# Graph attention in another order on VectorE and GpSimd, scores in two pairs of PSUM banks, and a mixer with ScalarE taps and full-width skip products

## The chip, the core and the metric

The kernel is one program on one core of a Trainium2 chip. TensorE (PE) does matrix products into PSUM, VectorE (DVE) and ScalarE (ACT) work elementwise, GpSimd (POOL) does elementwise work and issues indirect DMAs, and SyncE (SP) issues the other transfers. The engines run side by side and meet at semaphores. The metric is the device time of the core in microseconds (us), the median of the runs.

## What is computed

The input is `x` of 8 graphs x 1024 nodes x 128 features with an adjacency matrix of 1024x1024 each. Four blocks add to it: a graph convolution, a mixture of experts, the attention over graphs below, and a slicing block with a mixer. Two of them are touched.

```python
# attention block, per graph: 4 heads of 32, node_feats = layernorm(x)
X = heads(lrelu(node_feats @ W_lin + b_lin)); q = heads(lrelu(node_feats @ W_q)); k = heads(lrelu(node_feats @ W_k))
adj_h = adj[:, None] * sigmoid(q @ k.T * hd ** -0.5)
deg = sum(adj_h, -1); dis = where(deg > 0, deg ** -0.5, 0)
Y = (dis[..., :, None] * adj_h * dis[..., None, :]) @ X        # then layernorm(Y) * ln_g + ln_b
# mixer, inside the slicing block: 8 sequences of 64 steps, 8 heads of 64
xBC = silu(sum(xp[:, k:k + L] * conv_w[:, k] for k in range(3)) + conv_b)      # causal, 3 taps
h = h * exp(dt * A) + dt * B * x;  y = h @ C                   # scan, both directions
y = y + x_og * repeat(x_og @ fcD_w.T + Dp, 64)                 # the skip
yg = y * silu(z);  out = rms(yg) * norm_w @ out_w.T
```

## The kernel before

The stages run one after the other: convolution and experts up to about 666 us, `attention_gnn_stage` to about 1206, slicing, `hydra_stage` (the mixer) from about 1388 to 1475, and the way back to nodes.

**Attention.** A graph is 16 steps n: two halves of 512 queries by 8 tiles of 128 keys. In step g (over all graphs) TensorE does, in this order: `products` of the step 18 earlier (L1327, into YA), `scores` (L1314, four heads of 32 rows side by side in the array, into the one PSUM tile S of four banks), `degrees` of the step two earlier (L1341), and at most one side job out of the table `SIDE`: the projections k, q and x, transposes of X and Y, all through the one PSUM bank M. ScalarE makes AH (128x2048) with one sigmoid over S (L1417); the next scores wait for it (`att_ready`). VectorE multiplies AH by the adjacency tile A (L1447). AH has 18 buffers and A four. Beside the multiply VectorE has the small work of a graph in an order written out by hand, by n: the leaky functions of q, k and x (L1532, L1543), the degrees (L1490), XT = XR scaled by the degrees (L1500, `scale_X`), the statistics of the next X (`stats_x`, at step 4 for graphs 0 and 1, else at the start; for the first three graphs it adds the two gathered halves first, L1453 and L1455), and the norm of Y of the graph two earlier: `scale_Y` L1508, `stats_y`, `gain_Y`, `finish`.

GpSimd's order in a graph i: four gathers of graph i+2 (`gather`, L1242, indirect DMAs of routed expert rows), the reciprocal root of the variance of X (`norm_in.power`, L136), `root` of the degrees' second half (L1234), four gathers, R plus shift (L1287), `norm_y.power`, eight gathers, `root` of the first half, and `combine` (L1251, L1254), which adds the gathered halves and X for graph i+2 where i+2 is at least 3.

**Mixer.** TensorE projects the input, VectorE adds the three taps of the causal convolution (`convolve`, L2250 to L2254) for BC and four tiles of X, the decays go through ScalarE (L2209) and a transfer to DRAM and back into `decay`, whose ends GpSimd clears (L2090). VectorE scans twice (L2312, L2317), multiplies by G in 16 pieces (L2321), adds both directions (L2326) and applies the skip (L2332). The skip's products (L2141) take two columns of `fcD` at a time, each broadcast to 64 columns of the array, by four tiles of X.

## Time and profile before

| | us |
|---|---|
| median of 3 runs | 1538.24 (1538.18 to 1538.66) |
| the profiled execution | 1539.02 |
| its span, first to last instruction | 1537.30 |
| attention stage within it (666 to 1206) | 540 |
| mixer within it (1388 to 1475) | 87 |

The time is that of the whole launch; the profile shows one execution, 0.78 us above the median, with 1.72 us outside its span. TensorE is busy 91% of the span, VectorE 66%, ScalarE 49% and GpSimd 47%. The granted TensorE clock is 0.984 on average. Starts are in us from the span's start.

### The profile page before, as it was taken

The numbers are of one execution on the slowest core, as the hardware profiler recorded it, in microseconds if no ns is written. First come the engines' busy times: TensorE is split into PE (matmuls) and PEld (weight loads), VectorE is DVE, ScalarE is ACT, GpSimd is POOL, SyncE is SP. The second block draws the span as 40 slices with busy tenths as digits, with TensorE's granted clock in tenths as the row PEclk, the third lists the DMA queues.
The fourth block names the chain that finished last, engine by engine and source line by source line (L and its number), as shares of the span: only waits on it lengthen the run. The fifth ranks groups of instructions, "written<-read, shape, count | busy, mean of one in ns | idle before, by whom it ended". The sixth has DMA issues, their size and how long they took to land. (4 is left out here: it accounts for less than half of the span.)

```text
span 1537.3 us, 25067 instructions
## 1 busy us (share of the span) xinstructions
PE 1401.7 (91%) x9010; PEld 808.8 (53%) x9010; DVE 1021.2 (66%) x2212; ACT 748.2 (49%) x1184; POOL 720.7 (47%) x500
## 2 busy tenths in 40 slices
PE   4999999899999999977899988998999779999998
PEld 2455545669999998732222222222222357773488
DVE  2467767633333333368788999999987789967732
ACT  3365565534444444446454554655554457872110
POOL 1127776740000000749787887876233479981000
PEclk9999999999999999999999999999999999999999
DMA  9757637276788775633342424423322231004024
GB/s 300 254 188 282 235 118 228 88 205 203 229 230 231 233 228 159 171 118 125 96 129 90 124 84 122 142 84 119 91 90 69 69 95 42 15 1 90 1 85 138
DMA packets 207599, 215.26 MB, mean 140 GB/s; under 512 B 23269, under 2 KB 164709, under 8 KB 207476
## 3 DMA queue, kind: packets, MB, share of 16 engines
q1 hardware_dynamic: 199284, 196.81, 41.9%
q0 software_dynamic: 8192, 16.86, 3.5%
q8 instruction: 72, 1.18, 0.3%
q14 instruction: 51, 0.42, 0.1%
HBM read 168.54 MB, written 45.07 MB: 139 GB/s over the span
## 5 line engine op out<-in xcount | busy, mean ns | idle before, releaser
L1417 ACT ACTIVATE c_AH<-c_S 128x2048 f32<-128x2048 f32 x128 | 240.6, 1879 | 235.5 <-PE c_S L1314 235.5
L1447 DVE TENSOR_TENSOR c_AH<-c_AH,c_A 128x2048 f32<-128x2048 f32 x128 | 313.0, 2454 | 44.2 <-ACT c_AH L1417 43.9
L1242 POOL DMA_INDIRECT G<-ys,slots x102 | 195.4, 1915 | 32.7 <-issue 28.0
L810 ACT ACTIVATE a_A<-a_DG,a_A 128x256 f32<-128x256 f32 (+1 forms) x192 | 93.8, 527 | 208.3 <-PE a_DG L677 207.0
L530 POOL DMA_INDIRECT rows<-a_S,a_slots x128 | 134.0, 1047 | 49.9 <-issue 38.1
L557 POOL DMA_INDIRECT a_A<-ys,slots x16 | 16.4, 1024 | 292.9 <-DMA ys<-a_A 288.3
L1341 PE MATMUL c_DG<-c_AH,c_ones 128*32 128x512 f32 x1024 | 138.1, 612 | 12.0 <-DVE c_AH L1447 12.0
L1327 PE MATMUL c_YA<-c_AH,c_XT 128*32 128x512 f32 x1024 | 137.9, 620 | 12.1 <-DVE c_XT L1500 12.1
L1314 PE MATMUL c_S<-c_Q,c_K 32*128 32x512 f32 x928 | 135.2, 653 | 14.5 <-DVE c_K L1532 7.8
L648 PE MATMUL a_AG<-a_A,x 128*128 128x512 f32 x256 | 114.1, 599 | 5.1 <-DVE a_Z L891 5.1
L677 PE MATMUL a_DG<-a_A 128*128 128x256 f32 (+1 forms) x336 | 99.9, 420 | 7.1 <-ACT a_A L810 6.0
L690 PE MATMUL a_AG<-a_A 128*128 128x128 f32 x848 | 102.9, 277 | 0.0
L690 PEld LDWEIGHTS a_AG<-a_A 128*128 128x128 f32 x848 | 99.8, 194 | 3.5 <-issue 3.4
L1314 PEld LDWEIGHTS c_S<-c_Q,c_K 32*128 32x128 f32 x928 | 36.9, 186 | 116.6 <-ACT c_AH L1417 52.8
L690 PE MATMUL a_TP<-a_A 128*128 128x128 f32 x800 | 96.3, 275 | 0.0
L690 PEld LDWEIGHTS a_TP<-a_A 128*128 128x128 f32 x800 | 93.2, 192 | 2.9 <-issue 2.9
L1234 POOL TENSOR_TENSOR c_raw<-c_deg,c_power 128x16 f32<-128x16 f32 x16 | 73.0, 4562 | 36.0 <-DVE c_deg L1490 35.8
L677 PE MATMUL a_FG<-a_A 128*128 128x256 f32 (+1 forms) x312 | 86.0, 398 | 0.0
L648 PEld LDWEIGHTS a_AG<-a_A,x 128*128 128x128 f32 x256 | 47.3, 190 | 69.5 <-issue 59.4
L985 DVE COPY a_A<-a_AG 128x256 f32<-128x256 f32 x71 | 30.1, 424 | 75.0 <-PE a_AG L658 75.0
L1341 PEld LDWEIGHTS c_DG<-c_AH,c_ones 128*32 128x32 f32 x1024 | 20.4, 108 | 112.2 <-issue 83.8
L1697 POOL TENSOR_TENSOR s_SW<-s_SW,s_top 128x512 f32<-128x512 f32 x64 | 67.0, 1048 | 25.7 <-DVE s_top L1883 25.3
(393 smaller groups left out, 2566.2 us busy)
## 6 DMA issues: line engine op xcount, KB each, us to landing
a_A<-in_dram SPq DMA_DIRECT2D x72, 578.0 KB, 4.0
a_A<-in_dram SPq DMA_DIRECT2D x32, 1024.0 KB, 10.0
c_A<-in_dram SPq DMA_DIRECT2D x128, 256.0 KB, 2.8
a_A<-rows SPq DMA_DIRECT2D x71, 129.0 KB, 3.3
ys<-a_A SPq DMA_DIRECT2D x71, 128.0 KB, 2.3
a_X<-in_dram SPq DMA_DIRECT2D x8, 512.0 KB, 13.0
a_R<-in_dram SPq DMA_DIRECT2D x8, 512.0 KB, 5.3
stream<-a_R SPq DMA_DIRECT2D x8, 512.0 KB, 10.0
```

The lines of the kernel that those rows point to most:

```text
L530: pool.indirect_dma_start(rows, bass.IndirectOffsetOnAxis(ap=slots[:, k, T * i + t:T * i + t + 1], axis=0), S[i % 3][k][:, t, :], None, bo ...
L648: mm = pe.matmul(AG[:, half(h)], F[:, t, :], adj(i)[:, t, half(h)], start=(t == 0), stop=(t == T - 1))
L677: pe.matmul(up_bank(g, f)[:, 0:n], w_of(g)[:, f * P:(f + 1) * P], xT_of(g)[:, 0:n], start=True, stop=True).then_inc(up_psum, 1)
L690: mm = pe.matmul(YB[g % 2][:, t, :], hT[g % 2][:, f, t * P:(t + 1) * P], w_of(g)[:, F_N + FT + f * D:F_N + FT + (f + 1) * D], start=(f == ...
L810: act.activation(hT[g % 2][:, f, 0:size(g)], up_bank(g, f)[:, 0:size(g)], ACT.Gelu, bias=w_of(g)[:, F_N + f:F_N + f + 1]).then_inc(h_ready, 1)
L1234: pool.tensor_tensor(raw[:, tiles(half), :], deg[:, tiles(half), :], power[:, :].rearrange("p (t h) -> p t h", h=HEADS)[:, tiles(half), :] ...
L1242: pool.indirect_dma_start(Gt[k][:, t, :], None, ys, bass.IndirectOffsetOnAxis(ap=slots[:, k, T * i + t:T * i + t + 1], axis=0), bounds_che ...
L1314: mm = pe.matmul(S[:, h, :], keys[rows, t * P:(t + 1) * P], queries[rows, :], start=True, stop=True)
L1327: mm = pe.matmul(YA[h * HD:(h + 1) * HD, half, :], XT[:, t, h * HD:(h + 1) * HD], ah[:, h, :], start=(t == 0), stop=(t == T - 1))
L1341: mm = pe.matmul(DG[h * HD:(h + 1) * HD, :], ones[:, :], ah[:, h, :], start=(t == 0), stop=(t == T - 1))
L1417: act.activation(AH[g % UNITS][:, :, :], S[:, :, :], ACT.Sigmoid, scale=HD ** -0.5).then_inc(att_ready, 1)
L1447: dve.tensor_tensor(ah[:, :, :], ah[:, :, :], A[g % ADJ_BUFS][:, :].unsqueeze(1).to_broadcast([P, HEADS, HALF]), ALU.mult).then_inc(ah_dve, 1)
```

## The change

In the attention: `stats_x` of graph 2 moves from step 4 to 5 of graph 1, with `apply_x` two steps behind it. The tile S becomes S0 and S1 for two heads each, with semaphores of their own, and the sigmoid becomes two activations of 128x1024. On VectorE `leak_qk` of k moves ahead of the multiply of step 1, `scale_X` of the second half ahead of `stats_x`, `stats_y` from step 5 to behind the multiply of step 8, `gain_Y` from step 8 to halves at 10 and 11, and `finish` from 9 to 13. On GpSimd two gathers move ahead of the first norm, `norm_y.power` behind four more gathers, and `root` ahead of the last four. In the mixer the first tap with the bias moves to ScalarE, the skip's weights are widened by GpSimd copies to 128x512 so that 16 products of full width replace 32 of half width, and the 16 products by G become one instruction. Line numbers of the changed kernel are 8 higher in the attention's VectorE part.

```diff
@@ -28,7 +28,7 @@
 DVE_SUMS = 3
-STATS_AT = (4, 4)
+STATS_AT = (4, 5)
 ROUTED = 2 * TOK // G + E_N - 1
...
@@ -1132,7 +1133,7 @@
 
-        S = ps("S", [P, HEADS, HALF])
+        S = [ps(f"S{p}", [P, PAIR, HALF]) for p in range(2)]
         YA = ps("YA", [P, NH, HALF])
...
@@ -1255,8 +1256,9 @@
             combine(1)
+            gather(2, range(2))
             norm_in.power(pool, power, 0, 0)
-            gather(2, range(10))
+            gather(2, range(2, 10))
             root(0, 0)
...
@@ -1285,13 +1287,15 @@
                     pool.tensor_tensor(R[:, :, :], R[:, :, :], wide(shift), ALU.add).then_inc(shifted, 1)
+                gather(i + 2, range(8, 12))
+                if is_graph(i - 2) and i - 2 < B - 1:
                     norm_y.power(pool, power, i - 2, i % 2)
                 if i == B - 1:
                     pool.wait_ge(temp_max, 1)
                     pool.tensor_tensor(temp[:, :], temp[:, :], minus[:, :], ALU.pow).then_inc(temp_ready, 1)
-                gather(i + 2, range(8, 16))
                 if is_graph(i):
                     root(i, 0)
+                gather(i + 2, range(12, 16))
                 if is_graph(i + 2):
...
@@ -1308,11 +1312,12 @@
                 queries = YT[:, 0:HALF] if i == 0 and half == 0 else Q[:, cols(half)]
-                wait(pe, att_ready, g)
-                for h in range(HEADS):
-                    rows = slice(h * HD, (h + 1) * HD)
-                    mm = pe.matmul(S[:, h, :], keys[rows, t * P:(t + 1) * P], queries[rows, :], start=True, stop=True)
-                mm.then_inc(s_psum, 1)
+                for p in range(2):
+                    wait(pe, att_ready[p], g)
+                    for h in range(p * PAIR, (p + 1) * PAIR):
+                        rows = slice(h * HD, (h + 1) * HD)
+                        mm = pe.matmul(S[p][:, h % PAIR, :], keys[rows, t * P:(t + 1) * P], queries[rows, :], start=True, stop=True)
+                    mm.then_inc(s_psum[p], 1)
 
...
@@ -1412,9 +1417,11 @@
                     if is_graph(i):
-                        act.wait_ge(s_psum, g + 1)
                         wait(act, y_psum, g - UNITS + 1)
-                        act.activation(AH[g % UNITS][:, :, :], S[:, :, :], ACT.Sigmoid, scale=HD ** -0.5).then_inc(att_ready, 1)
+                        for p in range(2):
+                            act.wait_ge(s_psum[p], g + 1)
+                            act.activation(AH[g % UNITS][:, p * PAIR:(p + 1) * PAIR, :], S[p][:, :, :], ACT.Sigmoid,
+                                           scale=HD ** -0.5).then_inc(att_ready[p], 1)
                     if n == 0 and is_graph(i):
...
@@ -1442,7 +1449,8 @@
                 dve.wait_ge(adj_loaded[g % ADJ_BUFS], 16 * (g // ADJ_BUFS + 1))
-                dve.wait_ge(att_ready, g + 1)
+                for p in range(2):
+                    dve.wait_ge(att_ready[p], g + 1)
                 ah = AH[g % UNITS]
...
@@ -1513,14 +1521,14 @@
 
-            def gain_Y(i):
-                for t in range(T):
+            def gain_Y(i, half):
+                for t in range(4 * half, 4 * half + 4):
                     ins = dve.scalar_tensor_tensor(out=Y[:, t, :], in0=Y[:, t, :], scalar=norm_y.mean[i % 2][:, t:t + 1],
                                                    in1=gain[:, :], op0=ALU.subtract, op1=ALU.mult)
                 ins.then_inc(yg_ready, 1)
 
             def finish(i):
-                dve.wait_ge(yg_ready, i + 1)
+                dve.wait_ge(yg_ready, NH * i + NH)
                 dve.wait_ge(shifted, i + 1)
...
@@ -1557,17 +1565,17 @@
                         read_degrees(i, 0)
+                    if n == 1 and is_graph(i):
+                        leak_qk(K, i, "k1")
                     if is_graph(i):
                         multiply(STEPS * i + n)
+                    if n == 4 and is_graph(i - 1):
+                        scale_X(i - 1, 1)
                     if n == stats_step(i) and i < B:
                         stats_x(i + 1)
-                    if n == 1 and is_graph(i):
-                        leak_qk(K, i, "k1")
                     if n == 2 and is_graph(i):
                         leak_qk(Q, i, "q1")
-                    if n == 4 and is_graph(i - 1):
-                        scale_X(i - 1, 1)
-                    if n == (6 if i < len(STATS_AT) else 4) and is_graph(i + 1):
+                    if n == (stats_step(i) + 2 if i < len(STATS_AT) else 4) and is_graph(i + 1):
                         apply_x(i + 1)
...
@@ -1575,11 +1583,11 @@
                         read_fold()
-                    if n == 5 and is_graph(i - 2) and i - 2 < B - 1:
+                    if n == 8 and is_graph(i - 2) and i - 2 < B - 1:
                         stats_y(i - 2)
-                    if n == 8 and is_graph(i - 2) and i - 2 < B - 1:
-                        gain_Y(i - 2)
-                    if n == 9 and is_graph(i - 2) and i - 2 < B - 1:
+                    if n in (10, 11) and is_graph(i - 2) and i - 2 < B - 1:
+                        gain_Y(i - 2, n - 10)
+                    if n == 13 and is_graph(i - 2) and i - 2 < B - 1:
                         finish(i - 2)
...
@@ -2086,9 +2096,12 @@
             pool.wait_ge(decay_loaded, 32)
-
             pool.memset(decay[:, 0:SH, :, 0:1], 0.0).then_inc(ends_ready, 1)
             pool.memset(decay[:, SH:DTS, :, G_N - 1:G_N], 0.0).then_inc(ends_ready, 1)
+            pool.wait_ge(z_psum, KT)
+            for k in range(KT):
+                pool.tensor_copy(skipw[:, k, :, :].rearrange("p c (q d) -> p c q d", q=2),
+                                 fcD[:, :, 2 * k:2 * k + 2].unsqueeze(3).to_broadcast([P, KT, 2, SP_])).then_inc(skip_w, 1)
             pool.wait_ge(consts, 2)
...
@@ -2136,11 +2149,9 @@
                 pe.wait_ge(z_ready, k + 1)
-                for q in range(2):
-                    for c in range(KT):
-                        mm = pe.matmul(Z_[k][q * SP_:(q + 1) * SP_, :],
-                                       fcD[:, c, 2 * k + q:2 * k + q + 1].to_broadcast([P, SP_]), XC[:, c, :],
-                                       start=(c == 0), stop=(c == KT - 1))
+                pe.wait_ge(skip_w, k + 1)
+                for c in range(KT):
+                    mm = pe.matmul(Z_[k][:, :], skipw[:, k, c, :], XC[:, c, :], start=(c == 0), stop=(c == KT - 1))
                 mm.then_inc(fcd_psum, 1)
...
@@ -2203,10 +2214,20 @@
             act.activation(tmp[1], tmp[1], ACT.Exp, scale=-1.0).then_inc(e_ready, 1)
+
+            def tap(out, src, k, ready, count):
+                act.wait_ge(ready, count)
+                act.activation(out, src, ACT.Identity, bias=cb[:, k:k + 1], scale=cw[:, k, 2:3]).then_inc(first_tap, 1)
+
+            act.wait_ge(halved, 1)
+            tap(BC[:, :], BC_[:, :], KT, bc_psum, 1)
             act.wait_ge(u_ready, 1)
             act.activation(tmp[3], tmp[2], ACT.Ln).then_inc(ln_ready, 1)
+            tap(XC[:, 0, :], X_[0][:, :], 0, x_psum, 1)
             act.wait_ge(dts_ready, 1)
             act.activation(dA, dts, ACT.Exp, scale=A[:, :]).then_inc(dA_ready, 1)
+            for k in range(1, KT):
+                tap(XC[:, k, :], X_[k][:, :], k, x_psum, k + 1)
             act.wait_ge(bc_conv, 1)
...
@@ -2245,9 +2266,8 @@
 
-            def convolve(out, src, w, bias, done):
-
-                link(dve.tensor_scalar(out, src, w[:, 2:3], bias, ALU.mult, ALU.add))
+            def convolve(out, src, w, done):
+
                 o, x = by_graph(out), by_graph(src)
...
@@ -2295,8 +2317,8 @@
             for k in range(KT):
-                dve.wait_ge(x_psum, k + 1)
-                convolve(XC[:, k, :], X_[k][:, :], cw[:, k, :], cb[:, k:k + 1], x_conv)
+                dve.wait_ge(first_tap, k + 2)
+                convolve(XC[:, k, :], X_[k][:, :], cw[:, k, :], x_conv)
             dve.wait_ge(bc_tanh, 1)
...
@@ -2317,10 +2339,8 @@
             dve.wait_ge(g_psum, 1)
-            for j in range(DTS):
-                ins = dve.tensor_tensor(decay[:, j, :, :], decay[:, j, :, :],
-                                        G_[:, 0:BP * G_N].rearrange("p (b l) -> p b l", b=BP), ALU.mult)
-            link(ins)
+            g_all = G_[:, 0:BP * G_N].rearrange("p (b l) -> p b l", b=BP).unsqueeze(1).to_broadcast([P, DTS, BP, G_N])
+            link(dve.tensor_tensor(decay, decay, g_all, ALU.mult))
             by_hb = lambda a, lo, hi: a.rearrange("p h b l -> p (h b) l")[:, :, lo:hi]
```

The order on VectorE, graph 5 of the kernel before, from the multiply of step 5 on:

```order
L1447 TENSOR_TENSOR c_AH<-c_AH,c_A 128x2048
L124 BN_STATS c_yst<-c_Y 128x6 x8
L126 TENSOR_TENSOR c_ysums<-c_yst 128x16
L127 TENSOR_TENSOR c_ydm<-c_yst 128x8
L128 TENSOR_SCALAR c_ymean<-c_ysums 128x8
L129 SCALAR_TENSOR_TENSOR c_ydm<-c_ydm 128x8
L131 TENSOR_SCALAR c_yvar<-c_ysums 128x8
L132 TENSOR_TENSOR c_yve<-c_yvar,c_ydm 128x8
L1543 TENSOR_TENSOR c_XR<-c_M,c_bias 128x512
L1532 SCALAR_TENSOR_TENSOR c_XR<-c_XR 128x512
L1447 TENSOR_TENSOR c_AH<-c_AH,c_A 128x2048
```

The same place in the changed kernel:

```order
L1455 TENSOR_TENSOR c_AH<-c_AH,c_A 128x2048
L1551 TENSOR_TENSOR c_XR<-c_M,c_bias 128x512
L1540 SCALAR_TENSOR_TENSOR c_XR<-c_XR 128x512
L1455 TENSOR_TENSOR c_AH<-c_AH,c_A 128x2048
L1551 TENSOR_TENSOR c_XR<-c_M,c_bias 128x512
L1540 SCALAR_TENSOR_TENSOR c_XR<-c_XR 128x512
L1455 TENSOR_TENSOR c_AH<-c_AH,c_A 128x2048 x2
L124 BN_STATS c_yst<-c_Y 128x6 x8
```

The statistics of Y stood between the multiply of step 5 and the read of the x projection; now they stand three multiplies later.

The order on GpSimd in a graph of the kernel before, from `norm_in.power` on:

```order
L136 TENSOR_TENSOR c_irstd<-c_ive,c_power 128x8
L1234 TENSOR_TENSOR c_raw<-c_deg,c_power 128x16
L1242 DMA G<-ys,slots 128x128 x4
L1287 TENSOR_TENSOR c_R<-c_R,c_shift 128x1024
L136 TENSOR_TENSOR c_yrstd<-c_yve,c_power 128x8
L1242 DMA G<-ys,slots 128x128 x8
L1234 TENSOR_TENSOR c_raw<-c_deg,c_power 128x16
L1251 TENSOR_TENSOR G<-G 128x1024
L1254 TENSOR_TENSOR x<-x,G 128x1024
```

The same place in the changed kernel:

```order
L136 TENSOR_TENSOR c_irstd<-c_ive,c_power 128x8
L1235 TENSOR_TENSOR c_raw<-c_deg,c_power 128x16
L1243 DMA G<-ys,slots 128x128 x4
L1289 TENSOR_TENSOR c_R<-c_R,c_shift 128x1024
L1243 DMA G<-ys,slots 128x128 x4
L136 TENSOR_TENSOR c_yrstd<-c_yve,c_power 128x8
L1235 TENSOR_TENSOR c_raw<-c_deg,c_power 128x16
L1243 DMA G<-ys,slots 128x128 x4
L1252 TENSOR_TENSOR G<-G 128x1024
L1255 TENSOR_TENSOR x<-x,G 128x1024
```

The root moved ahead of the last four gathers, so the sum of the halves now follows the last gather directly; `norm_y.power` has four more gathers before it.

## Rows read from the trace of the kernel before

**Rows 1.** Busy time by windows: columns as in the header; graphs 1, 4 and 6.

```profile
core 0: us, PE busy (x) PEld busy (x) DVE busy (x) ACT busy (x) POOL busy (x), PEclk, DMA share, GB/s
723.10:791.00 67.90, 59.22 (x416) 15.48 (x416) 54.42 (x57) 34.90 (x25) 56.65 (x30) 0.95 0.33 100
...
923.80:990.00 66.20, 60.32 (x434) 16.94 (x435) 61.66 (x87) 35.38 (x26) 55.24 (x24) 0.97 0.37 112
...
1057.20:1119.40 62.20, 60.43 (x432) 16.32 (x433) 56.06 (x87) 35.39 (x26) 15.74 (x5) 0.97 0.35 103
```

**Rows 2.** Timeline of a bare step: start, us, engine, line, work [idle before <-releaser].

```profile
1039.50 1.14 PE L1314 MATMUL c_S<-c_Q,c_K 32*128 32x512 f32 x8
...
1042.64 0.31 PEld L1314 LDWEIGHTS c_S<-c_Q,c_K 32*128 32x128 f32 x8 [1.06 <-ACT c_AH L1417]
```

**Rows 3.** Timeline of graph 1, from the scores of step 5 on.

```profile
740.34 1.14 PE L1314 MATMUL c_S<-c_Q,c_K 32*128 32x512 f32 x8
...
742.60 1.22 DVE L1453 TENSOR_TENSOR G<-G 128x1024 f32<-128x1024 f32 x1
...
748.48 1.93 PE L1327 MATMUL c_YA<-c_AH,c_XT 128*32 128x512 f32 x8 [6.01 <-DVE c_XT L1500]
```

**Rows 4.** Timeline of graph 4, steps 6 to 8.

```profile
948.20 4.70 DVE L1447 TENSOR_TENSOR c_AH<-c_AH,c_A 128x2048 f32<-128x2048 f32 x1
948.36 2.38 POOL L1287 TENSOR_TENSOR c_R<-c_R,c_shift 128x1024 f32<-128x1024 f32 x1
...
950.83 1.14 PE L1314 MATMUL c_S<-c_Q,c_K 32*128 32x512 f32 x8
...
955.97 2.07 PE L1370 MATMUL c_M<-W,xnT 128*128 128x128 f32 x8 [1.94 <-DVE c_XR L1543]
...
959.43 1.14 PE L1314 MATMUL c_S<-c_Q,c_K 32*128 32x512 f32 x8
```

**Rows 5.** Timeline of graph 5, from step 14 to the next graph's first.

```profile
1047.73 6.65 DVE L1447 TENSOR_TENSOR c_AH<-c_AH,c_A 128x2048 f32<-128x2048 f32 x2
1047.76 4.46 POOL L1251 TENSOR_TENSOR G<-G 128x1024 f32<-128x1024 f32 x1
...
1054.30 2.82 DVE L1532 SCALAR_TENSOR_TENSOR c_K<-c_K 128x512 f32<-128x512 f32 x1
...
1057.17 1.38 PE L1314 MATMUL c_S<-c_Q,c_K 32*128 32x512 f32 x8 [4.28 <-DVE c_K L1532]
```

**Rows 6.** Page part 5, costliest groups: gathers and sigmoid (busy, mean ns | idle, releaser).

```profile
L1417 ACT ACTIVATE c_AH<-c_S 128x2048 f32<-128x2048 f32 x128 | 240.6, 1879 | 235.5 <-PE c_S L1314 235.5
...
L1242 POOL DMA_INDIRECT G<-ys,slots x102 | 195.4, 1915 | 32.7 <-issue 28.0
```

**Rows 7.** Timeline of GpSimd in graph 5, its wait for the Y statistics.

```profile
1021.58 1.66 POOL L136 TENSOR_TENSOR c_yrstd<-c_yve,c_power 128x8 f32<-128x8 f32 x1 [4.64 <-DVE c_yve L132]
```

**Rows 8.** DMA issues: median us from issue to landing, an indirect transfer.

```profile
rows<-a_S,a_slots POOLq DMA_INDIRECT x128, 2.6
```

**Rows 9.** Groups by shape, ScalarE: an activation of 128x1024 out of PSUM.

```profile
L1800 ACT ACTIVATE carry<-s_TP 128x1024 f32<-128x1024 f32 x4 | 4.1, 1026 | 3.1 <-PE s_TP L98 3.1
```

**Rows 10.** Timeline of TensorE within 959.40 to 959.50: first passes of four heads.

```profile
959.43 0.71 PE L1314 MATMUL c_S<-c_Q,c_K 32*128 32x512 f32 x4
```

**Rows 11.** Timeline of the mixer: GpSimd, VectorE and TensorE.

```profile
1406.93 0.79 DVE L2250 TENSOR_SCALAR h_XC<-h_K,h_cw,h_cb 128x512 f32<-128x512 f32 x1
...
1421.63 0.15 POOL L2090 MEMSET M<- 128x32 f32 x1 [23.73 <-DMA M<-dA_rows]
...
1423.58 4.42 DVE L2312 TENSOR_TENSOR_SCAN M<-M,h_inx 128x2048 f32<-128x2048 f32 x1
...
1426.27 16.06 PE L2141 MATMUL h_K<-h_XC,h_fcD 128*64 128x512 f32 x64
...
1435.88 5.38 DVE L2321 TENSOR_TENSOR M<-M,h_K 128x256 f32<-128x256 f32 x16
...
1443.65 2.72 DVE L2332 SCALAR_TENSOR_TENSOR h_XC<-h_K,h_Dc,h_XC 128x512 f32<-128x512 f32 x4
```

11 lines of the change are left out of this document (8 added, 3 removed).

## The prediction

> **What bounds the kernel now.** I read the windows by graph first, then the timeline of TensorE for steps that are longer than their work, and then what stood on the engine that released the wait. In a steady graph (4) TensorE is busy 60.3 of 66.2 us, VectorE 61.7, GpSimd 55.2 and ScalarE 35.4 [rows 1]. None is full; TensorE waits in few places, each time for small VectorE work, and that work waits behind GpSimd or behind something longer on VectorE itself. A bare step takes 3.14 us from scores to scores, and it ends when ScalarE gives S back [rows 2].
>
> Three stalls show the pattern. In graph 1 the products of step 6 wait 6.01 us for XT, which stands on VectorE behind the sums and the statistics of graph 2's X: they end at 748.48 + 1.93 = 750.4, so the step that began at 740.34 takes 10 us where a bare one takes 3.14 [rows 2, 3]. The granted clock of that graph is 0.95 [rows 1]: part of it ran at 1.2 in place of 2.4 GHz after this wait. In graph 4 a multiply takes 4.70 us beside GpSimd's R plus shift of 2.38, so that 2.32 is its own, the statistics of Y follow, the read of the x projection comes late, and the step takes 959.43 - 950.83 = 8.60 us [rows 4]. At the end of graph 5 two multiplies and the leaky function of k share the time with the two sums of `combine` on GpSimd, and TensorE waits 4.28 us for K [rows 5]. A VectorE or a GpSimd instruction with two inputs from SBUF waits for the other's to end; that is how I read rows 4 and 5.
>
> **Is GpSimd a bound of its own?** Its busy 55.24 us in graph 4 [rows 1] and 16 gathers with 0.3 us of issue ahead of each (28.0 us over 102 [rows 6]) make 55.24 + 4.8 = 60.0 us. The rest of 66.2 is waiting, the longest piece 4.64 us for the statistics of Y [rows 7]. So a graph can't be shorter than some 60 us of GpSimd, and graph 6, where it has almost nothing to do (15.74), takes 62.2 us: TensorE's own length with a few stalls left is 60 to 62 [rows 1].
>
> **The change, part by part.** Sums are made against the profiled 1539.02; the median is 0.8 lower.
>
> *Graph 0 and the split.* Two activations in place of one cost 2 x 1.026 = 2.05 in place of 1.88 us [rows 6, 9], 0.17 a step on ScalarE, which has 30 us free in a graph. What the split gives: the first pair's scores may start while ScalarE reads the second pair. In graph 0, which has few products, steps hang on that loop (3.14) and VectorE (multiply 2.32 and small work) is the next bound; I take -2 us, between -4 (16 steps at 0.25) and +1. Later, the second pair of a step with products is given back 2.05 + 1.2 = 3.25 us after its start, against 3.14 - 0.06 before: up to +0.15 in each of the four bare steps of a graph and nothing where a side job fills the time. Over 7 graphs that is 7 x 4 x 0.15 = 4 at most; most graphs have another bound, so +1.5.
>
> The rows bear on one more question of the split. Four heads' first passes start inside one 0.1 us window [rows 10], so tiles of the array run side by side in the records, and two pairs without a wait between them should do as well. The Trainium skill ("TensorE: Matmul & The Clock Gate", Part 3, "The mechanism") says that matmuls start and end in program order; by that rule a second pair held up by its own semaphore holds up everything behind it. The same part's "The cost: per-tile semaphore tail" gives about 26 ns for one more increment; no row here prices it, and by that figure the second increment would add 128 x 0.026 = 3.3 us at most (an estimate).
>
> *Graph 1.* The step of 10 us goes back to about 3.1 when XT is made ahead of the sums, and the lower clock after it costs no more: 8 us. The two sums (1.22 each), the statistics and then `apply_x` of graph 2 still stand on VectorE, now at steps 5 to 7, with the x projections and the transposes of step 8 and 9 behind them; I take 5 of the 8 us back: -3. On GpSimd the sums for graph 3 now come after all gathers and root, and must wait for the last gather to land (2.6 us, the nearest row [rows 8]); they end about 5 us later than before, but graph 2 no longer starts late on K's account: -4. Graph 1 with its join to 2: -7, of which graph 0's 2 is apart.
>
> *Graphs 2 to 5.* In graph 4 the multiply and the statistics of Y no longer stand before both x projections: the step of 8.60 returns to about 4.1. The lock on the multiply beside R plus shift may stay (GpSimd's work is the same) but what follows it is 2 us shorter, so 3 of 4.5 go. The waits of GpSimd for Y's statistics vanish, since power now stands behind four more gathers; its cycle is 60.0 + 2.6 for the landing = 62.6. VectorE's is 61.7 busy, of which 2.4 is blocked in rows 4 and about 2.0 + 2.1 in rows 5, TensorE's 60.3 plus stalls. The highest, 62.6, is what I take for graphs 3, 4 and 5 against 66.2: 3 x -3.6 = -10.8, and 0.5 more for graph 5's longer wait [rows 5]: -11.3. Graph 2 begins with X late from graph 1's `combine` and gets only -0.6. Graph 6 has no gathers and loses the statistics' stall alone, 62.2 - 60.4 = 1.8 of waiting at most [rows 1]: -1.4. Graph 7 has that stall too, and `scale_X` ahead of the last statistics: between 1.4 and 4 (a wait as in rows 5), -2.5. Cover: should `combine` slide further behind the graph's end, it runs into k1's leaky function as in rows 5; I hold it there for one graph, +1.
>
> Attention: -2 + 1.5 - 7 - 0.6 - 11.3 - 1.4 - 2.5 + 1 = -22.3.
>
> *Mixer.* VectorE loses five first taps of 0.79 [rows 11] = 4.0, and 16 pieces in 5.38 become one of 128x4096; by the multiply of 128x2048 in 2.32 it takes 4.5 to 4.6: 0.9. Not all of it is worth time: the first scan can't start before `decay` has come from DRAM and its ends are cleared, at 1421.8, while the scan starts at 1423.58, 1.8 us after that [rows 11]. The transfer starts after ScalarE's exponent, which depends on the softplus and moves by 0.8 at most. So the scans come 0.8 + 1.7 = 2.5 earlier, and with the 0.9 the skip (1443.65) could start 3.4 earlier, at 1440.2. TensorE's skip products, 16.06 us from 1426.27 for 64 records of half the array [rows 11], become 32 of the full one. Two halves side by side took 16.06 / 32 = 0.50; a second pass of the scores ends 1.14 - 0.71 = 0.43 after the first [rows 4, 10]. So they end between 1440.0 and 1442.3; I take 0.43, as nothing is halved any more. Both meet at 1440.3: -3.3 (-1.3 by the other end). The four copies on GpSimd (128x512) stand before those products and have 20 us of room. Bounds: -4.9 if the decay also comes earlier, -1 if a copy collides with the scan (4.4 us) and is not ready.
>
> **Sum.** 1539.02 - 22.3 - 3.3 = 1513.4; less the 0.8 to the median and rounded, **1513.0**.
>
> **Rivals.** *(A) GpSimd and the lock bound more than I take.* Every sum, root and power blocks VectorE and is blocked by it, and with a denser VectorE the gathers grow: their mean is 1.92 [rows 6]; at 2.1 each the cycle is 16 x 0.2 = 3 us longer, 4 graphs x 3 = 12 of the 22 us go, hence 1513 + 12 = 1525. For it: rows 1 show GpSimd at 55 to 57 in any graph. Against it: the waits of 6 us take up the first of it. *(B) GpSimd doesn't bind.* The landing is hidden, since combine has a graph's start as slack, and graphs take 60.5, the length of TensorE's busy time: 4 x 2.3 more: 1503. *(C) The other side: the second pair starts only after the first one's passes.* If the array doesn't overlap the two pairs (separate tiles, separate semaphores and waits in between), each step is longer by a pass, 0.43 to 0.55 us. TensorE's graph grows from 60.3 by 16 x 0.5 less the slack of four bare steps (2) to 66.3, with 1 us of stalls 67.3, above every other bound, where the seven graphs from 723.10 to about 1180 took 65.3 on average: 7 x 2 + 2 in graph 0 - 3.3 in the mixer = +12.7, 1551. It decides from the point where a pair's first record starts more than 0.3 us after the other's with both semaphores given. Rows 10 speak against it. By the rule in "The mechanism" the two may still start together; only a late semaphore of the second pair costs anything. *(D) Stalls only move.* K against `combine`, as in rows 5, at the end of each graph, 4 us times 5, and the mixer's gain alone stays with a little: 1536.
>
> **How the numbers follow.** My case 0.52; (A) 0.18; (B) 0.17; (C) 0.08; (D) 0.05. A measurement of this kernel can tell 0.2% (3.1 us) from no change. Faster by more: my case, A, B = 0.87, less 0.01 for what lies between; within: D's larger half and the edge of A, 0.05; slower: C and a bit of the unforeseen, 0.09. My case spans 1504 to 1522 (graph 0 and the split 5 us, the cycle 62.6 give or take 1.5 times four, mixer 2). The range takes in most of A and B: 1500 to 1527.
>
> **What would show it.** Right: in graph 1 no wait above 2 us for XT; graphs 3 to 5 of 62 to 63.5 us with GpSimd's wait for Y's statistics gone; bare steps 3.1 to 3.3; the skip at about 1440 less what came earlier; in the mixer no wait of TensorE for the widened weights. Wrong: two pairs of scores 0.4 us or more apart in the records (C); GpSimd without waits and a graph above 64 (A); a wait of the scores for K at each graph's start (D); graphs at 60.5 (B).

## The result: 10 us faster, less than half of what was forecast

The changed kernel takes 1528.11 us (median of 4 runs, 1526.99 to 1531.31) against 1538.21 (1537.93 to 1538.66; four runs taken with it): the ratio is 0.9937, with an interval of 0.992 to 0.9955. I forecast 1513 and a range of 1500 to 1527; the time lies just above it. The sign was right, the size was less than half. The ratios below, though not the medians, leave out the runs recorded as slow (one of e15 at 2838 us, one of e4, two of the kernel before).

The executions differ in the stages ahead of the attention, which no edit touches: the first scores start at 670.72 us in the profiled execution of after (1531.31 us, span 1529.24) and at 666.30 in that of before, and in the sets of e1 to e4 and e13 to e16 they start at 692 to 704, in old and new kernels alike. So from here on the attention is measured by one stretch of the TensorE timeline, **from the start of the first scores to the start of the last** (128 steps), and the rest by the stretch from there to the end. The first repeats to 0.4 us in the one pair of traces that can show it: 512.7 before, 513.1 in e4, where the attention is the same. It is read from one execution of each kernel, so a difference of less than a microsecond is not shown by it. The second does not repeat so well: with the mixer of the changed kernel it is 354.1 to 357.9 in the thirteen traces.

| us | before | after | forecast of the difference |
|---|---|---|---|
| first to last scores | 512.7 | 503.8: -8.9 | -22.3 |
| last scores to the end | 358.3 | 354.7: -3.6 | -3.3 |

By graph (start to start; the last to its sixteenth scores), after minus before: -2.1, +0.1, -0.1, +1.2, 0.0, -4.0, -0.7, -3.3. I had said -2, -7, -0.6, three times -3.8, -1.4 and -2.5, with +1.5 for the split and +1 as cover. A "join" below is the last step of a graph, up to the first scores of the next; "low clock" is TensorE at 1.2 in place of 2.4 GHz for a while, which shows as a granted clock below 1.00.

The busy time of each engine in graphs 1, 4, 5 and 6 of the changed kernel, by windows (columns as in rows 1):

```profile
core 0: us, PE busy (x) PEld busy (x) DVE busy (x) ACT busy (x) POOL busy (x), PEclk, DMA share, GB/s
725.44:793.50 68.06, 59.48 (x416) 16.62 (x417) 52.38 (x57) 35.97 (x41) 40.55 (x23) 0.95 0.32 99
927.38:993.52 66.14, 61.04 (x433) 17.16 (x433) 62.28 (x87) 36.35 (x42) 49.52 (x24) 0.97 0.37 112
993.52:1056.67 63.15, 59.44 (x433) 16.94 (x433) 61.40 (x87) 36.35 (x42) 50.51 (x24) 1.00 0.38 117
1056.67:1118.21 61.54, 60.97 (x433) 17.18 (x433) 58.57 (x87) 36.35 (x42) 17.19 (x6) 0.97 0.34 104
```

GpSimd's busy time fell from 55.2 to 49.5 us in graph 4 [rows 1], and the graph is as long as before. The waits of TensorE in the attention (engine, tile and line that waited, what it waited for; total us, times, longest):

```profile
PE c_S L1319 <- DVE c_K L1540: 11.9, 6, 2.2
PE c_M L1375 <- DVE c_Y L1516: 7.1, 3, 2.4
PE c_YA L1332 <- DVE c_XT L1508: 6.6, 8, 2.3
PE c_DG L1346 <- DVE c_AH L1455: 6.0, 5, 3.0
PE c_M L1372 <- DVE x L142: 4.6, 1, 4.6
```

Two stalls are gone: the wait for XT in graph 1 (6.01 us, [rows 3]) and the read of the x projection behind the Y statistics [rows 4]. Two have come: the scaling of Y in graphs 2 to 4, and x in graph 1. One has grown: K, which TensorE waited 0.9 us for at four joins of the kernel before and 4.28 at one [rows 5], and now 2.2 at each of the joins into graphs 2 to 6.

**The new wait for K**, at the end of graph 4, from the timelines of GpSimd, VectorE and TensorE:

```profile
970.80 3.68 POOL L136 TENSOR_TENSOR c_yrstd<-c_yve,c_power 128x8 f32<-128x8 f32 x1 [9.97 <-DVE c_yve L132]
...
989.25 3.66 POOL L1252 TENSOR_TENSOR G<-G 128x1024 f32<-128x1024 f32 x1 [2.07 <-DMA G<-ys,slots]
...
990.62 2.84 DVE L1540 SCALAR_TENSOR_TENSOR c_K<-c_K 128x512 f32<-128x512 f32 x1
...
993.52 1.14 PE L1319 MATMUL c_S<-c_Q,c_K 32*128 32x512 f32 x8 [2.20 <-DVE c_K L1540]
```

GpSimd's wait for the Y statistics has not gone, it has doubled: 9.97 us in graph 4, where it was 4.6 in each of graphs 2 to 5 before [rows 7]. Its gathers go through faster (1.66 us on average, 1.92 in rows 6; in graph 4 the sixteen take 26.3 us instead of 32.3, which is all of the fall in its busy time), the statistics come three steps later, and so it idles. Behind that wait stand root, the last four gathers and their landing (2.07), and the first sum of `combine` then starts while VectorE is at the multiply of step 14. K's leaky function comes next; it takes 2.84 us instead of 0.68, and TensorE waits 2.20.

**The new wait for Y**, step 6 of the same graph: the shift of R now meets `apply_x`, eight pieces in 5.15 us (2.13 free), and the x projection waits for the bank that Y is read from:

```profile
950.84 5.15 DVE L142 TENSOR_SCALAR x<-x,c_imean,c_irstd 128x128 f32<-128x128 f32 x8
...
952.34 2.36 POOL L1289 TENSOR_TENSOR c_R<-c_R,c_shift 128x1024 f32<-128x1024 f32 x1
...
956.48 1.16 PE L1375 MATMUL c_M<-W,xnT 128*128 128x128 f32 x8 [2.37 <-DVE c_Y L1516]
```

The step takes 6.59 us, where before one of 8.59 stood. This wait comes with the split alone: e3, with the old orders, has it at four steps (9.5 us). **In graph 1** the wait for XT shrank to 1.11, and the transpose of step 8 waits for `apply_x` instead, in a step of 9.65 us where one of 10.01 had been:

```profile
745.75 1.06 PE L1332 MATMUL c_YA<-c_AH,c_XT 128*32 128x512 f32 x8 [1.11 <-DVE c_XT L1508]
...
762.51 1.09 PE L1372 MATMUL c_M<-ident,x 128*128 128x128 f32 x4 [4.62 <-DVE x L142]
```

**The mixer** (timeline of its end; the last scores are 4.48 us earlier than in rows 11, so 4.48 comes off each start before it is compared):

```profile
1414.78 0.16 POOL L2099 MEMSET M<- 128x32 f32 x1 [21.08 <-DMA M<-dA_rows]
...
1418.83 2.80 POOL L2103 COPY h_inz<-h_fcD 128x512 f32<-128x512 f32 x4 [3.83 <-PE h_K L2113]
...
1421.62 13.90 PE L2154 MATMUL h_K<-h_XC,h_inz 128*128 128x512 f32 x32
...
1427.43 4.42 DVE L2343 TENSOR_TENSOR M<-M,h_K 128x4096 f32<-128x4096 f32 x1
...
1435.56 2.73 DVE L2352 SCALAR_TENSOR_TENSOR h_XC<-h_K,h_Dc,h_XC 128x512 f32<-128x512 f32 x4 [1.24 <-PE h_K L2154]
```

The 32 products take 13.90 us (13.8 forecast), the one product by G 4.42 (4.5), and the skip comes 1443.65 - 1435.56 - 4.48 = 3.6 us earlier. It waits 1.24 us for TensorE, so the products set its start.

But not all of the 3.6 is the change's. From the mixer's first instruction to the skip it takes 55.6 us in the trace of before, 54.3 in each of the four other traces with the old mixer (e3, e5, e6, e9) and 52.1 in all thirteen with the new one. In the trace of before the decays came back from DRAM late: their ends are cleared 33.6 us after the mixer's start, in all other traces, old mixer or new, 31.2 to 31.6 after it. In e3, where they were in time, the old mixer's skip waited for its products too (start of the mixer, clearing, skip):

```profile
1421.41 0.10 POOL L2087 MEMSET h_power<- 128x8 f32 x1 [10.46 <-POOLq L1612]
...
1452.65 0.16 POOL L2095 MEMSET M<- 128x32 f32 x1 [21.02 <-DMA M<-dA_rows]
...
1475.74 2.73 DVE L2337 SCALAR_TENSOR_TENSOR h_XC<-h_K,h_Dc,h_XC 128x512 f32<-128x512 f32 x4 [0.87 <-PE h_K L2146]
```

So the change is worth 2.2 us here, the products' 16.06 - 13.90, and the other 1.3 is an accident of the trace that the forecast was read from. VectorE's own savings make it ready 2.6 us earlier (53.5 to 50.8 us after the mixer's start): without them the skip would have waited for VectorE, at 53.5.

### The profile page after: what moved, and what is told of

It reads as the page before. It is cut to its first block and busy times, and to the rows that moved or that the text cites. A ratio compares the mean times of both kernels' runs of the same rounds, so it can differ in the third digit from the quotient of the medians.

```text
span 1529.2 us, 25127 instructions
## 1 busy us (share of the span) xinstructions
PE 1411.4 (92%) x8978; PEld 818.4 (54%) x8978; DVE 1015.3 (66%) x2192; ACT 759.5 (50%) x1317; POOL 687.9 (45%) x504
## 5 line engine op out<-in xcount | busy, mean ns | idle before, releaser
L1423 ACT ACTIVATE c_AH<-c_S 128x1024 f32<-128x1024 f32 x256 | 248.3, 1022 | 212.8 <-PE c_S L1319 212.8
L1455 DVE TENSOR_TENSOR c_AH<-c_AH,c_A 128x2048 f32<-128x2048 f32 x128 | 308.4, 2412 | 40.7 <-ACT c_AH L1423 39.6
L1243 POOL DMA_INDIRECT G<-ys,slots x102 | 169.6, 1663 | 47.5 <-issue 26.9
L1319 PE MATMUL c_S<-c_Q,c_K 32*128 32x512 f32 x928 | 143.7, 655 | 12.2 <-DVE c_K L1540 11.9
L1319 PEld LDWEIGHTS c_S<-c_Q,c_K 32*128 32x128 f32 x928 | 43.4, 186 | 112.5 <-issue 72.3
L1705 POOL TENSOR_TENSOR s_SW<-s_SW,s_top 128x512 f32<-128x512 f32 x64 | 66.8, 1044 | 25.3 <-DVE s_top L1891 24.8
L810 ACT ACTIVATE a_A<-a_FG,a_A 128x256 f32<-128x256 f32 (+1 forms) x156 | 74.0, 494 | 2.4 <-PE a_FG L677 2.4
```

What stands on the lines that cost most here:

```text
L810: act.activation(hT[g % 2][:, f, 0:size(g)], up_bank(g, f)[:, 0:size(g)], ACT.Gelu, bias=w_of(g)[:, F_N + f:F_N + f + 1]).then_inc(h_ready, 1)
L1243: pool.indirect_dma_start(Gt[k][:, t, :], None, ys, bass.IndirectOffsetOnAxis(ap=slots[:, k, T * i + t:T * i + t + 1], axis=0), bounds_che ...
L1319: mm = pe.matmul(S[p][:, h % PAIR, :], keys[rows, t * P:(t + 1) * P], queries[rows, :], start=True, stop=True)
L1423: act.activation(AH[g % UNITS][:, p * PAIR:(p + 1) * PAIR, :], S[p][:, :, :], ACT.Sigmoid, scale=HD ** -0.5).then_inc(att_ready[p], 1)
L1455: dve.tensor_tensor(ah[:, :, :], ah[:, :, :], A[g % ADJ_BUFS][:, :].unsqueeze(1).to_broadcast([P, HEADS, HALF]), ALU.mult).then_inc(ah_dve, 1)
L1705: pool.tensor_tensor(SW[k][:, :, :], SW[k][:, :, :], top[n % 3][:, :].unsqueeze(2).to_broadcast([P, SH, G_N]), ALU.subtract).then_inc(cent ...
```

## The experiments

Of each kernel: the median against the kernel before in the same set of runs, with the ratio and its interval, and the stretch from first to last scores in its profile. The whole times of e3, e4 and e6 can't be told from the kernel before (their intervals include 1); what is said of them rests on one trace each. "Free" is 0.68 for K's function and 2.29 for a multiply.

### Which part brings what

The four parts of the change, each alone on the kernel before.

```diff
+        S = [ps(f"S{p}", [P, PAIR, HALF]) for p in range(2)]      # scores in two pairs, e3
```

> Edit on the kernel before: the scores in two pairs of banks, with two sigmoids and two semaphores, nothing else. From the changed kernel's steps (2.92 and 4.41 where 3.14 and 4.12 stood, graph 0 54.7 instead of 56.8): graph 0 gains 1 to 2 us, the other graphs nothing: -2 to +1 against the kernel before. Rival C (the second pair starts behind the first one's passes): +30 us or more. Rival S (shorter sigmoids of a pair, 0.97 us, let VectorE start earlier everywhere): -5.

1567.06 against 1571.15 us (ratio 0.9982, 0.9959 to 1.0004); first to last scores **508.4**: -4.3. Graph 0 takes 54.7 and not 56.8 (expected), and each of graphs 1, 6 and 7 some 0.4 to 0.9 less (not expected). A bare step takes 2.92 and the one with a side job behind it 4.41, together 7.33, where 3.14 + 4.12 = 7.26 stood: no gain in steady steps. Rival C is dead: in the changed kernel's TensorE timeline within 0.1 us, two heads of S0 and two of S1 start together, as four of S did in rows 10:

```profile
985.11 0.71 PE L1319 MATMUL c_S<-c_Q,c_K 32*128 32x512 f32 x4
```

In three steps of each of graphs 1 to 7 the second pair starts 0.30 us after the first, beside the first one's pass of 0.53 and not behind it. There the second sigmoid of the step before ends 0.25 us after the first pair's start, so it is a late semaphore.

> Edit on the kernel before: the changes in the mixer only (first tap on ScalarE, skip weights widened by GpSimd, 16 full-width products, one product by G). The changed kernel's time from the last scores of the attention to the end is 354.7 us against 358.3: -3.6. Theory: -3.3 to -3.7 against the kernel before, all of it here. Rival: part of the 3.6 is due to what the attention leaves behind (its last steps end earlier): then -2 or less.

1567.07 against 1571.15 (0.9987, 0.9959 to 1.0014); first to last scores 513.1, last scores to the end **354.6**: -3.7 against the trace of before, but -2.7 against e3, run in the same set. By the mixer's own stretch it is -2.2 (above). The gain does not come from the attention; its size is 2.2 and not the 3.3 to 3.7 I expected.

```diff
+                gather(i + 2, range(8, 12))
+                if is_graph(i - 2) and i - 2 < B - 1:
                     norm_y.power(pool, power, i - 2, i % 2)
...
-                gather(i + 2, range(8, 16))
                 if is_graph(i):
                     root(i, 0)
+                gather(i + 2, range(12, 16))                       # GpSimd's order, e5
```

> Edit on the kernel before: GpSimd's order alone (norm_y.power behind gathers 8 to 12, root ahead of the last four, two gathers ahead of the first norm), VectorE's order and the single S unchanged. Measured by the stretch from the first to the last scores in the trace: 512.7 before, 503.8 in the changed kernel, 508.4 with the split alone. Theory V (VectorE's chain of small work between steps 8 and 15 is full, and every input-locked microsecond of GpSimd's sums lengthens it wherever they stand): statistics of Y are early here, so GpSimd doesn't wait; the sums slide by the landing (2 us) towards K: 511 to 515. Rival G (the order on GpSimd is what brings the gain): 505 or less.

1538.49 against 1541.5 (0.9969, 0.9947 to 0.9991); first to last scores **512.3**, as theory V had it. GpSimd waits 7.2 us a graph for the degrees (root stands ahead of the last gathers) instead of 4.6 for the statistics.

```diff
-                    if n == 5 and is_graph(i - 2) and i - 2 < B - 1:
+                    if n == 8 and is_graph(i - 2) and i - 2 < B - 1:
                         stats_y(i - 2)                             # and the rest of VectorE's order, e6
```

> Edit on the kernel before: VectorE's order alone (statistics of Y behind step 8, gain in halves at 10 and 11, finish at 13, K ahead of the multiply of step 1, XT ahead of the statistics), GpSimd's order and the single S unchanged. Here eight gathers stand behind norm_y.power, which waits for the late statistics. Theory V with GpSimd pinned: eight gathers, root and sums after step 8 end some 8 us later than now, in the next graph's first steps, its statistics of X come late: 515 to 530 from first to last scores. Rival: VectorE's order alone brings what the split alone does not (4.6 us): 508.

1540.11 against 1541.5 (0.9988, 0.9966 to 1.001); first to last scores **512.4**. Neither of my numbers: not 515 or more, not 508. GpSimd waits 11.0 us a graph for the statistics, its sums fall into the next graph's first steps, where step 1 takes 6.1 us (4.12 free), and the joins become free (3.24). Stalls moved and summed to the same.

So the parts bring 4.3 + 0.4 + 0.3 = 5.0 us alone and 8.9 together; the 0.4 and the 0.3 are no more than the repeat of 0.4 and can't be told from nothing.

### What makes K late

```diff
-                gather(i + 2, range(8, 12))
+                gather(i + 2, range(8, 16))
                 ...
-                gather(i + 2, range(12, 16))
```

> Edit on the changed kernel: GpSimd issues all of gathers 8 to 16 ahead of norm_y.power, where four of them stood behind it. Theory G (GpSimd idles about 10 us for the statistics of Y, so root, the last gathers, their landing and the two sums of combine end at the next graph's start and block K's leaky function): power and root end at the same time as now, combine starts some 9 us earlier (landing hidden), the scores of a graph's first step no longer wait for K (2.2 us six times, and the low clock after it, 5.7 instead of 4.1): graphs 2 to 6 some 3 us shorter each, in all 12 to 16 us below the changed kernel, about 1514. Rival F (K is late because finish now stands ahead of it on VectorE): no difference, 1527. Rival M (the sums of combine block whatever VectorE does wherever they stand): the waits move into the steps 11 to 14, no more than 3 us gained.

1565.93 against 1571.15 (0.9973, 0.9949 to 0.9996); first to last scores **511.5**: 7.7 us *worse* than the changed kernel, by one trace each. Theory G fell: nothing of the 12 to 16 us came. The sums come earlier indeed, 16.2 us ahead of the next graph's scores where it was 4.3, and K's own function is free at the joins into graphs 3 to 6, but (timelines of GpSimd, VectorE, TensorE at the end of graph 4):

```profile
1003.83 3.15 POOL L1252 TENSOR_TENSOR G<-G 128x1024 f32<-128x1024 f32 x1
...
1004.67 5.43 DVE L1525 SCALAR_TENSOR_TENSOR c_Y<-c_Y,c_ymean,c_gain 128x128 f32<-128x128 f32 x4
...
1019.33 0.68 DVE L1539 SCALAR_TENSOR_TENSOR c_K<-c_K 128x512 f32<-128x512 f32 x1
...
1020.06 1.14 PE L1318 MATMUL c_S<-c_Q,c_K 32*128 32x512 f32 x8 [2.86 <-DVE c_K L1539]
```

the second half of the gain takes 5.43 us instead of 1.13, and K, 14 us later, is late by 2.86. VectorE never makes the 4.3 us good. That led to **theory Q**: from the multiply of step 8 through K's function VectorE has seven multiplies (16.0), the statistics of Y (2.5), the degrees (0.3), the gain (2.3), Q (0.7), finish (2.2) and K (0.7), in all 24.7 us, and TensorE's steps 8 to 14 take 25.3. By the theory a lock anywhere in this queue arrives at K (a "lock" is an instruction held by one on the other engine).

```diff
-                    if n == 13 and is_graph(i - 2) and i - 2 < B - 1:
+                    if n == 12 and is_graph(i - 2) and i - 2 < B - 1:
                         finish(i - 2)
```

> Edit on the changed kernel: finish of Y (8 pieces, 2.2 us) one step earlier, behind the multiply of step 12 instead of 13, so that it is out of the way of K's leaky function. Theory G (K is blocked by the first sum of combine on GpSimd, 2.84 us instead of 0.68): no difference, within 2 us of the changed kernel, the wait for K of 2.2 us stays in six graphs. Rival F (K is late because of finish): the wait goes, 6 x (2.2 + 1.6 of low clock) = up to 20 us less, near 1508.

1564.18 against 1571.15 (0.995, 0.9917 to 0.9983); first to last scores **511.6**. Rival F fell, and "no difference" was wrong too: finish came ahead of Q and of the multiply of step 13, two multiplies ran into the sums (6.66 us for two), and K, held itself (2.82), is late by 4.13 instead of 2.20 at the joins into graphs 4 to 6 (2.20 still at the two before). By whole time neither e1 nor e2 can be told from the changed kernel, whose interval (0.992 to 0.9955) overlaps both:

```profile
1011.43 6.66 DVE L1455 TENSOR_TENSOR c_AH<-c_AH,c_A 128x2048 f32<-128x2048 f32 x2
...
1018.01 2.82 DVE L1540 SCALAR_TENSOR_TENSOR c_K<-c_K 128x512 f32<-128x512 f32 x1
...
1020.89 2.09 PE L1319 MATMUL c_S<-c_Q,c_K 32*128 32x512 f32 x8 [4.13 <-DVE c_K L1540]
```

Without the first sum (combine leaves out the second expert's half):

> Edit on the changed kernel that leaves work out: combine adds only the first gathered half to X (the sum of the two halves on GpSimd, 3.7 us, is left out, so x lacks the second expert from graph 3 on). Theory L: the sum that stood beside K's function is gone, GpSimd's other sum (2.7 us) now stands where it did; if it still meets K, the wait shrinks to 1 us, if not it goes: 490 to 497 from first to last scores. Rival V: what counts is the number of locked microseconds on VectorE, one of the two blocks of 2.2 us goes from five graphs: 11 us plus the low clock: 490. Rival G (position of combine behind the Y statistics is all that counts): 500 or more.

1525.52 against 1541.5 (0.9901, 0.9873 to 0.9929); first to last scores **499.6**. Without the first sum K is no better off: TensorE still waits 2.2 us for it at five joins, because the other sum now meets it (its function takes 2.84), and the 4 us come from steps elsewhere. 499.6 lies outside what theory L (490 to 497) and rival V (490) gave and next to what G gave (500 or more), so it singles out none of them; L's "shrinks to 1 us" was wrong.

```diff
+                dve.scalar_tensor_tensor(out=K[:, 0:HALF], in0=M[:, :], scalar=0.01, in1=K[:, 0:HALF],
+                                         op0=ALU.mult, op1=ALU.max).then_inc(side_free, 1)
```

> Edit on the changed kernel: the leaky function of K's first half reads one input from PSUM (M) and only the other from SBUF, so that GpSimd's sums should not hold it (2.84 us now, 0.68 free). Theory L (the two-input sum on GpSimd holds a VectorE instruction with two SBUF inputs, and K is the one that TensorE waits for): K's function takes about 0.7 us, the wait of 2.2 us at the start of six graphs and the low clock behind it go: 3 to 3.8 us a graph, 15 to 20 in all, 485 to 490 from first to last scores. Rival V (the block moves to the next multiply, which lacks time then too): the wait for K goes but degrees wait for the multiply instead, 2 us a graph at most: 498 to 503. Rival: the instruction is held all the same: 504.

**1516.74** against 1541.5 (0.985, 0.9821 to 0.9878); first to last scores **489.8**, 14 less than the changed kernel. The same place as above, the end of graph 4, and the window of graph 4:

```profile
975.10 3.74 POOL L1252 TENSOR_TENSOR G<-G 128x1024 f32<-128x1024 f32 x1 [2.00 <-DMA G<-ys,slots]
...
976.55 0.68 DVE L1551 SCALAR_TENSOR_TENSOR c_K<-c_M,c_K 128x512 f32<-128x512 f32 x1
977.26 3.73 DVE L1458 TENSOR_TENSOR c_AH<-c_AH,c_A 128x2048 f32<-128x2048 f32 x1
977.33 1.14 PE L1321 MATMUL c_S<-c_Q,c_K 32*128 32x512 f32 x8
```

```profile
915.13:977.33 62.20, 59.52 (x432) 16.97 (x433) 60.78 (x87) 36.36 (x42) 49.63 (x24) 1.00 0.39 119
```

The function starts 1.4 us into the sum and takes 0.68, here and at the four other joins beside a sum: with one operand in PSUM it isn't held. The multiply behind it is (3.73), and that costs TensorE 1.2 us in step 3 (4.81 for 3.65). The scores wait for nothing, and the granted clock of the graph is 1.00 where it was 0.97: a wait of some 2 us costs up to 1.6 more in the next step (5.71 in place of 4.12).

### Is it K's lock, or the queue ahead of K?

The same edit of K on three other kernels:

> Edit on the kernel before: K's first half takes its leaky function with one input from PSUM, nothing else. Theory L: the five joins of graphs that took 5.10, 3.83, 5.10, 5.10 and 7.28 us (3.23 where nothing waits), and the 5.71 after the last, go to 3.2 to 3.4 and 4.1: 512.7 - 11 = 502 from first to last scores, about 1528 in all where before has 1539. Rival (the statistics of Y ahead of the x projections is what bounds the old order, and it takes back what K gives): 508 or more.

1535.48 against 1543.82 (0.9956, 0.9929 to 0.9982); first to last scores **514.2**, where I had written 502. The profiled execution is the slowest of ten, 7.6 us above their median, and by the medians the edit brings 3 to 11 us, so "nothing" is what this trace shows and not what the times show. The trace has a reason: in the old order the sums start some 12 us ahead of the scores, and K's function was free (0.68) at every join but one already in the kernel before. What the sums hold is one multiply (3.17) and Q (2.85), the two multiplies behind are free (VectorE, end of graph 4):

```profile
980.65 3.17 DVE L1450 TENSOR_TENSOR c_AH<-c_AH,c_A 128x2048 f32<-128x2048 f32 x1 [1.83 <-ACT c_AH L1419]
983.74 2.85 DVE L1535 SCALAR_TENSOR_TENSOR c_Q<-c_Q 128x512 f32<-128x512 f32 x1
986.51 4.48 DVE L1450 TENSOR_TENSOR c_AH<-c_AH,c_A 128x2048 f32<-128x2048 f32 x2
990.91 0.68 DVE L1543 SCALAR_TENSOR_TENSOR c_K<-c_M,c_K 128x512 f32<-128x512 f32 x1
```

> The kernel before with the split scores, the mixer's changes and K from PSUM, but with the old orders on VectorE and GpSimd. The split alone has 508.4 from first to last scores with joins of 5.4 to 6.7 us. If the new orders are worth about 5 us once K is free: 495 (and 489.8 with them). If they are worth nothing: 490. If they are worth what their stalls in graphs 2 to 5 show (2 us a graph at step 7, and graph 1): 498 to 500.

1532.37 against 1543.82 (0.9921, 0.9896 to 0.9947); first to last scores **509.6**, worse than any of my three numbers, and 508.4 without the edit of K. By the stretches, freeing K is worth nothing with the old orders and 14 us with the new ones. So the orders are worth 509.6 - 489.8 = 19.8 us, once K is free. By the ratios (0.9921 and 0.985, in different sets) it is some 11 us, so the sign holds and the size is open.

> Edit on the version with K from PSUM: GpSimd issues gathers 8 to 16 ahead of norm_y.power, so that the sums come some 9 us earlier, beside the gain, Q and finish of VectorE. Theory L (only what TensorE waits for counts): K is no longer the victim; the sums leave steps 0 to 2 of the next graph, where degrees wait 1.1 us now, and meet Q and the multiply of step 12: 62.2 a graph gives 61 to 62: 483 to 489 from first to last scores. Rival V (VectorE's second half is full, so 4 us of lock there make K late whatever its operands): 495 or more, as 511.5 with K from SBUF.

1533.62 against 1543.82 (0.9925, 0.9899 to 0.9951); first to last scores **509.3**. Rival V, not theory L: the queue ahead of K is full, and K's own operands don't help.

The last four were run to settle this.

```diff
+                    if n == 14 and is_graph(i + 1):
+                        leak_qk(K, i + 1, "k0")
                     if is_graph(i):
                         multiply(STEPS * i + n)
```

> Edit on the changed kernel: K's leaky function (from SBUF, as it was) stands ahead of the multiply of step 14 instead of behind it. Theory Q (the sums of combine start at 989.25 in graph 4 and hold what VectorE has not yet done for K; what stands before them is free): K's function runs at about 988.4 to 989.1, just ahead of the first sum, takes 0.7 us, and the scores of a graph's first step wait for nothing: 488 to 492 from first to last scores, as with K from PSUM (489.8). Rival (the copy of K by ScalarE comes too late, or the first sum gets in between): the multiply of step 14 is late as well, 500 or more.

**1541.82** against 1571.53 (0.9834, 0.9789 to 0.9878); first to last scores **490.5**. Nothing but the order of two instructions, and it brings what the PSUM operand brought: 13.3 us against the changed kernel. K's function ends before the sum begins:

```profile
995.18 0.68 DVE L1540 SCALAR_TENSOR_TENSOR c_K<-c_K 128x512 f32<-128x512 f32 x1
...
996.08 4.21 POOL L1252 TENSOR_TENSOR G<-G 128x1024 f32<-128x1024 f32 x1 [2.03 <-DMA G<-ys,slots]
```

> Edit on the kernel with GpSimd's gathers ahead (511.5 from first to last scores, K waited for 2.9 us in five graphs): finish of Y (2.2 us of VectorE) at step 15, behind K, instead of 13. Theory Q (VectorE's queue from step 8 to K is full, so the 4.3 us that the gain is held by the sums make K late by 2.9): with 2.2 us less ahead of K the wait shrinks to 0.7 or less, the low clock behind it mostly goes: 492 to 500. Rival (K is late by the lock itself, wherever the queue stands): 508 or more.

1554.35 against 1571.53 (0.9909, 0.9882 to 0.9937); first to last scores **498.8**, 12.7 less than with finish in the queue. The waits of TensorE for K, of the kernel with the gathers ahead and of this one:

```profile
PE c_S L1318 <- DVE c_K L1539: 15.1, 6, 2.9
```

```profile
PE c_S L1318 <- DVE c_K L1539: 7.0, 6, 2.7
```

The early sums still hold Q (2.85) and two multiplies (6.67) ahead of K in graph 4, as much as they held the gain before, and K is now late by 0.8 to 0.9 at the joins into graphs 3 to 6 instead of 2.9; the 2.7 is the join into graph 2, where a sum still meets K itself. That is what theory Q said for 2.2 us of work taken out of the queue. Finish at step 15 was not run without the early sums, so what it would bring by itself is not shown.

### Graph 1, and the best version

```diff
-STATS_AT = (4, 5)
+STATS_AT = (4, 4)
```

> Edit on the version with K from PSUM: the sums and statistics of graph 2 at step 4 of graph 1 instead of 5, apply_x with them at 6. Step 8 of graph 1 takes 9.65 us there, since TensorE waits 4.6 us for x out of apply_x. Theory A (that chain on VectorE is what the step waits for, and one step earlier gives one step): the wait shrinks to about 2 us and the low clock goes: graph 1 at 61 to 63 us instead of 66.2. Rival B (the multiply behind the sums is late instead, degrees wait for it): graph 1 within 1 us of 66.2.

1511.71 (2 runs) against 1543.82 (0.979, 0.9723 to 0.9857); first to last scores **488.1**. Graph 1 takes 60.6 instead of 66.2 and the wait for x is gone; part of it comes back in graph 2, whose step 3 takes 7.65.

> Edit on the version with K from PSUM and the statistics of graph 2 at step 4: K's function also ahead of the multiply of step 14. Theory Q: K is in front of the sums either way, so the second way adds nothing: 487 to 489 as without it (488.1). Rival (some of the lock on the multiplies of steps 15 and 0 goes too): 484.

1544.28 against 1571.53 (0.9826, 0.9784 to 0.9868); **488.8**: the two ways for K don't add up, as expected.

> Edit on the changed kernel: K's function ahead of the multiply of step 14 and the sums and statistics of graph 2 at step 4 instead of 5, no operand changed. Both effects as in the runs before: 503.8 - 14 (K) - 5 (graph 1, 66.2 to 60.6) + 3 (graph 2, whose step 3 took 7.65 us there) = 488 from first to last scores, about 1512 on a chip where the kernel before has 1538. Rival: without the PSUM operand the sums still catch K in the graph where they come early: 495.

1543.86 against 1571.53 (0.9832, 0.9795 to 0.9868); **487.4**, the shortest attention in any trace. Two edits of the order in the changed kernel take another 16 us off the attention: by the stretches 1528 - 16 = 1512 us in the first set (worked out, not run; the versions with K freed and the statistics at step 4 can't be ranked, 487.4 to 488.8).

## Why the prediction was wrong

- **Graph 0 and the split: right.** -2.1 for -2, though graph 0 differs by some 1 us between traces of the same code (54.3 to 55.5 with the split, 56.5 to 57.2 without); the +1.5 for steady steps didn't show. Rival C didn't happen.
- **Graph 1: the step "I take 5 of the 8 us back" was too small.** The 8 us went and all of them came back: x out of `apply_x` (4.62, and 1 us of the next step), and K at the end. One step earlier for the statistics would have kept 5.6 of them (e10, with K freed).
- **Graphs 2 to 5: the first step that failed is "the waits of GpSimd for Y's statistics vanish, since power now stands behind four more gathers; its cycle is 60.0 + 2.6 for the landing = 62.6".** The wait rose to 9.97. I had moved the consumer by four gathers (6.6 us) and not set against it that the producer moved by three steps (some 11 us). And GpSimd's busy 55.2 was no fixed load: a gather takes 1.02 us where VectorE does nothing and up to 4.3 beside a multiply, and the sixteen of graph 4 fell by 6.0 us. That the wait alone was not what cost the time, e1 shows: with 1.6 us left of it in graph 4 the sums came 12 us earlier, and nothing was gained.
- **What cost the time is the cover: should `combine` slide further, "it runs into k1's leaky function as in rows 5; I hold it there for one graph, +1".** It slid, and it is k0's function that it meets, at five joins: TensorE waits 2.2 us at each, and in four cases up to 1.6 more in the next step at the low clock. With K out of the sum's way the same orders give 490.5 (e13) and 489.8 (e7), 13 to 14 us less. That is nearly all of the missing 13.4, and the attention then stands at the forecast's 512.7 - 22.3 = 490.4; that it fits so well is luck, since graph 1 still takes 65 to 66 us there, 5 more than I gave it, and graph 2 62.2, 3.5 less. So the forecast priced the graphs by the highest of three engines' sums and left out the order in which VectorE reaches K. That 62.6 is close to what the graphs take once K is free (62.2 to 62.7) is luck: GpSimd is busy 49.6 of them, so it doesn't set that length.
- **Rival (D), "stalls only move", had 0.05 and described the mechanism.** Its 1536 was too high because it left graphs 0, 5 and 7 nothing, where they gained 2.1, 4.0 and 3.3.
- **The lock beside R plus shift: "3 of 4.5 go" was 2.0** (8.59 to 6.59), with `apply_x` as the victim in place of the multiply.
- **The mixer: the number was met by luck,** -3.6 for -3.3. The product's length was right (13.9 for 13.8), but the sum took off from a skip at 1443.65 that a late transfer had put off by 1.3, and the "moves by 0.8 at most" for the decays was 0: their ends are cleared 31.2 to 31.6 us after the mixer's start with the old mixer and the new. Against the old mixer's usual trace the gain is 2.2.
- **What I didn't ask** was how much time VectorE has between one thing TensorE waits for and the next. The statistics moved out of a stretch with room into one that had 25.3 us for 24.7 of work.

What stays open: what the orders bring with the single S was not run; why the parts bring 5.0 alone and 8.9 together was not taken apart further, and why some joins are followed by a step at the lower clock and others (graph 5 of after) are not.
